# A Mamba layer on one core: ScalarE's carry copy and its exponential two states ahead, moved to the head of each slot

## The chip, the cores and the metric

One core of a Trainium2 chip runs the whole program. Its engines work side by side, each with a queue of its own that is executed in order: PE (TensorE, matrix products), DVE (VectorE), ACT (ScalarE), POOL (GpSimd), and SP (SyncE), which here only issues DMAs. They wait for one another through semaphores. The metric is the device time of one execution in microseconds, the median of several runs.

## The reference, cut to what matters

The input is x, 2 images of 512 channels x 4096 tokens in float32. Layer 0 is a group norm and a Mamba block, layer 1 a group norm and linear attention; both are residual. The change touches layer 0 only:

```
h0 = zeros                          # 1024 channels x 16 states
dA  = exp(d_t[..., None] * A)       # delta times A, for each channel and state
dBu = (d_t * u_t)[..., None] * b_t[:, None, :]
h   = dA * h + dBu
y   = einsum('bdn,bn->bd', h, c_t)
...
delta = softplus(dt @ dt_proj_w.T + dt_proj_b)
xn = (xf - mu) * rsqrt(var + EPS) * ln_w + ln_b
y = y * silu(z)
```

## The kernel before

**Tiling.** The 2 x 4096 tokens are cut into 16 chunks of T = 512 tokens. The 1024 inner channels are 8 tiles (j = 0 to 7) of 128 partitions, each with 16 states (n = 0 to 15). A chunk thus has 128 slots, slot = 16 j + n, and in each slot DVE runs one scan, `h = dA * h + dBu` along the 512 tokens of one tile and state (L638). Scan and slot have the same number here; "state 7 of tile 0" is slot 7. `chunk_loop` runs a body for chunks -1, 0, a loop over 1 to 14 (its body stands once in the program), 15 and 16. A body does three things at once: `scan` for chunk c, `front` for chunk c+1 (load of x, group norm, layer norm, input projection, convolution, softplus' input) and `project` for chunk c-1 (output projection, residual). Scan and front are both on for chunks 0 to 14.

**Order.** Every engine has a function of its own (`scalar_chunk`, `vector_chunk`, `gpsimd_chunk`, `tensor_chunk`) that walks through the 128 slots, and tables at the head of the file (NORM, RSTD = 24, NEWTON = 26, SP_LN = 5, Y_COPY = 2, and so on) say in which slot, or in which state of every tile, a piece of side work stands. So the queues' order is written by hand. Around a scan, in slot s:

- ACT (`scalar_chunk`) does the side work of the slot first. Then it copies the last column of scan s-1 into `carry` (L516; L520 for the first slot of a chunk), where the next chunk's scan of that tile and state begins; it waits for `h_ready`, that is for scan s-1. Then it computes exp(delta * A) for the scan of slot s+2 (L536), into SBUF (`da`, a ring of 3) or, for the six states whose dBu DVE computes, into one of three PSUM banks. The ring slot is free when scan s-1 is over, so this waits for the same scan.
- DVE does its side work, then the dBu product of the next state if that is one of the six (L625), then the scan. The scan waits for the exponential and for dBu.
- PE makes dBu for the other ten states, two slots ahead (L704, once scan s-1 is over), does its side work, and adds hc of slot s-2 into `y_ps` (L815).
- POOL multiplies each scan's result by C (L683: `hc`), between the sums of softplus and `du` (L651 to L669) and the gating (L676).

**ACT's side work**, with the lines of the profile:

- softplus for the next tile, in the states of each tile: Abs and Relu at 0 (L475, L479), Exp at 2 (L483), two roundings at 3 and 4 (L486, L490), Ln at 5 (L494). Ln lies in another table than Exp, so a table load stands before the Ln (L494) and another before the next exponential (L536);
- the copy of y out of PSUM at 2 (L506), which PE turns back (L713) for DVE's skip step (L594, state 4); before it PE must have summed state 15, and PE's sum of state 0 waits for the copy;
- the gate's Tanh at 9 (L510), between PE's product z (L787) and DVE's L588 (state 10); du_t at 13 (L498) and the copy of du at 15 (L502);
- for the next chunk: in slot 0 the issue of the load of x (L409), the group norm's scale at 4, 5, 9, 10 (L416), squares at 17 and 20 (L428), the layer norm's rstd as exp(-0.5 ln(var)) at 24 (L432, L434, with two table loads), which DVE refines by a Newton step at 26 (L552 to L560) and applies at 27 (L563); the affine step at 29 to 32 (L441); and for each of the eight tiles the convolution's first steps (L448 to L454) and its Tanh (L461), after PE's products (L757).

Slot 20 on DVE has the skip step of tile 0 and also adds the residual to one output tile (L601), with PE's output projection (L804, slots 0 to 36) behind both.

## Time and profile before

| | us |
|---|---|
| median of 3 runs | 5342.18 (5341.98 to 5363.9) |
| the profiled execution | 5340.43 |
| its span | 5338.7 |
| layer 0, scans of chunks 0 to 15 | from about 200 to about 4550 |
| layer 1 | the rest, to the end |

The page gives the busy time of each engine, the span in 40 slices and the costliest groups of instructions. Of the trace, these views are used: the waits (who waited for whom, in total), a table of busy times by stretch, and the instructions in order of time. There each row ends in brackets with the idle time of the engine just before it and what ended it. The granted TensorE clock is 0.97 over the span and 0.98 in the steady part of layer 0. One chunk takes 276 us there, and the chunks are alike.

### The profile page before, as it was taken

What the parts mean: (1) busy time and instruction counts of PE and PEld (TensorE: products, weight loads), DVE (VectorE), ACT (ScalarE), POOL (GpSimd) and SP (SyncE); (2) the same over time, 40 slices, a digit from 0 to 9 for tenths busy, and PEclk for the clock granted to TensorE, in tenths of its full rate; (3) what the DMA queues carried; (4) which work ended last, traced back from release to release, by engine and by line L of the source; (5) the groups of instructions that cost most, each with busy time, mean ns of one, the idle gap of its engine ahead of it and who ended that gap; (6) DMA issues with size and microseconds to landing.
All of it is one profiled execution on the core that took longest, in us unless ns stands there. A gap on an engine that the chain in (4) does not pass through costs nothing. (4 is left out here: it accounts for less than half of the span.)

```text
span 5338.7 us, 89822 instructions
## 1 busy us (share of the span) xinstructions
PE 4649.2 (87%) x26392; PEld 3406.2 (64%) x26392; DVE 3953.3 (74%) x4317; ACT 3672.1 (69%) x7235; POOL 3660.5 (69%) x2906
## 2 busy tenths in 40 slices
PE   2798989898989888989898989898898988798998
PEld 0566666666666666666666666666666667586786
DVE  4788878887888898888888888878788888212212
ACT  1677767677777776777777777767676767463563
POOL 1577777787777777777777787777777779332332
PEclk9999999999999999999999999999999999999999
DMA  5102020202020202010101010010102020322313
GB/s 188 52 2 68 2 67 3 65 5 65 5 65 5 61 9 61 9 57 13 57 13 57 13 39 31 28 42 12 58 2 68 1 64 1 111 67 92 113 56 110
DMA packets 119826, 245.63 MB, mean 46 GB/s; under 512 B 10496, under 2 KB 11648, under 8 KB 117728
## 3 DMA queue, kind: packets, MB, share of 16 engines
q1 hardware_dynamic: 110816, 222.30, 12.9%
q10 hardware_dynamic: 8448, 16.78, 0.9%
q8 instruction: 237, 3.88, 0.3%
q14 instruction: 325, 2.66, 0.2%
HBM read 204.44 MB, written 34.60 MB: 45 GB/s over the span
## 5 line engine op out<-in xcount | busy, mean ns | idle before, releaser
L683 POOL TENSOR_TENSOR hc<-hs,c_rows 128x512 f32<-128x512 f32 x2048 | 2626.2, 1299 | 996.9 <-DVE hs L638 930.9
L638 DVE TENSOR_TENSOR_SCAN hs<-da,carry,bank 128x512 f32<-128x512 f32 x1280 | 1623.0, 1268 | 133.0 <-PE bank L704 52.8
L704 PE MATMUL bank<-b_diag,du_t 128*128 128x128 f32 x10240 | 1414.1, 282 | 290.0 <-DVE hs L638 258.3
L815 PEld LDWEIGHTS bank<-identity,hc 128*128 128x128 f32 x8192 | 1010.6, 142 | 825.3 <-issue 720.2
L704 PEld LDWEIGHTS bank<-b_diag,du_t 128*128 128x128 f32 x10240 | 1269.4, 195 | 364.4 <-DVE hs L638 350.2
L815 PE MATMUL bank<-identity,hc 128*128 128x128 f32 x8192 | 1232.3, 276 | 58.7 <-ACT sp_l L506 39.4
L638 DVE TENSOR_TENSOR_SCAN hs<-bank,carry,hs 128x512 f32<-128x512 f32 x768 | 963.3, 1263 | 43.3 <-ACT bank L536 43.3
L536 ACT ACTIVATE da<-delta,neg_a 128x512 f32<-128x512 f32 x1280 | 910.7, 711 | 21.4 <-DVE hs L638 19.9
L516 ACT ACTIVATE carry<-hs,keep_now 128x1 f32<-128x1 f32 x2032 | 582.6, 287 | 327.1 <-DVE hs L638 320.9
L986 POOL TENSOR_TENSOR xg_low<-xg,xg_high 128x512 fp32r<-128x512 f32 x192 | 248.7, 1296 | 474.1 <-ACT xg_high L1010 466.6
L804 PE MATMUL bank<-xs,w_out 128*128 (+1 forms) x1024 | 520.5, 622 | 35.9 <-issue 34.3
L757 PE MATMUL bank<-xn,w_in 128*128 (+1 forms) x1024 | 524.8, 604 | 18.6 <-ACT xn L441 10.8
L625 DVE TENSOR_TENSOR hs<-bank,b_rows 128x512 f32<-128x512 f32 x768 | 518.2, 675 | 13.1 <-ACT carry L516 7.3
L787 PE MATMUL bank<-xn,w_in 128*128 (+1 forms) x1024 | 525.2, 595 | 0.0
L536 ACT ACTIVATE bank<-delta,neg_a 128x512 f32<-128x512 f32 x768 | 521.4, 679 | 0.5
L573 DVE SCALAR_TENSOR_TENSOR bank<-raw,w_conv,bank 128x512 f32<-128x512 f32 x384 | 288.4, 751 | 43.2 <-ACT bank L454 34.0
L804 PEld LDWEIGHTS bank<-xs,w_out 128*128 128x128 f32 x1024 | 180.7, 199 | 148.6 <-issue 143.5
L594 DVE SCALAR_TENSOR_TENSOR xs<-xs,skip,bank 128x512 f32 (+1 forms) x128 | 95.2, 744 | 220.8 <-PE bank L713 220.7
L651 POOL TENSOR_TENSOR sp_w<-sp_w,sp_e 128x512 f32<-128x512 f32 x128 | 163.4, 1276 | 136.0 <-ACT sp_w L490 136.0
L1010 ACT ACTIVATE xg<-xl,gn_bias,gn_scale 128x512 f32<-128x512 f32 x192 | 154.9, 807 | 138.3 <-DMA xl<-x 126.4
L510 ACT ACTIVATE zs<-bank 128x512 f32<-128x512 f32 x128 | 76.5, 597 | 233.9 <-PE bank L787 233.9
L1099 DVE COPY ek_t<-l_bank 128x512 f32<-128x512 f32 x64 | 44.3, 692 | 219.1 <-PE l_bank L1174 219.1
(157 smaller groups left out, 5987.8 us busy)
## 6 DMA issues: line engine op xcount, KB each, us to landing
c_rows<-b_and_c_rows SPq DMA_DIRECT2D x256, 256.0 KB, 3.4
xl<-x SPq DMA_DIRECT2D x48, 1024.0 KB, 5.6
b_rows<-b_and_c_rows SPq DMA_DIRECT2D x96, 256.0 KB, 3.7
c_rows<-in_x SPq DMA_DIRECT2D x8, 2048.0 KB, 8.5
xn<-in_x ACTq DMA_DIRECT2D x16, 1024.0 KB, 7.6
xres<-in_x SPq DMA_DIRECT2D x64, 256.0 KB, 2.9
x<-xres SPq DMA_DIRECT2D x64, 256.0 KB, 2.0
out<-keys SPq DMA_DIRECT2D x16, 1024.0 KB, 5.0
```

The costliest lines, as they stand in the source:

```text
L516: act.activation(carry[:, col:col + 1], hs[:, (n - 1) % H_RING, T - 1:T], ACT.Copy, scale=keep_now[:, 0:1]).then_inc(carried, 1)
L536: act.activation(x_ps[x][:, :] if nn in BY_VECTOR else da[:, x, :], delta[:, jn % 2, :], ACT.Exp, scale=neg_a[:, jn, nn:nn + 1]).then_inc( ...
L573: dve.scalar_tensor_tensor(in_ps[t % 2][:, :], raw[:, TAPS - 1 - s:TAPS - 1 - s + T], w, in_ps[t % 2][:, :], ALU.mult, ALU.add).then_inc(c ...
L625: dve.tensor_tensor(hs[:, nn % H_RING, :], du_ps[:, :], b_rows[:, v, :], ALU.mult).then_inc(dbu_ready, 1)
L638: dve.tensor_tensor_scan(hs[:, n % H_RING, :], decay, inflow, carry[:, STATE * j + n:STATE * j + n + 1], ALU.mult, ALU.add).then_inc(h_rea ...
L683: pool.tensor_tensor(hc[:, n % HC_RING, :], hs[:, n % H_RING, :], c_rows[:, n, :], ALU.mult).then_inc(hc_ready, 1)
L704: mm = pe.matmul(x_ps[target % STEPS % X_RING][:, q * P:(q + 1) * P], du_t[:, q * P:(q + 1) * P], b_diag[:, w, q, :], start=True, stop=True)
L757: mm = pe.matmul(in_ps[t % 2][:, :], w_in[:, ct, t * P:(t + 1) * P], xn[:, f % 2, ct, :], start=ct == 0, stop=ct == CT - 1)
L787: mm = pe.matmul(pb[:, :], w_in[:, ct, lo:lo + P], xn[:, c % 2, ct, :], start=ct == 0, stop=ct == CT - 1)
L804: mm = pe.matmul(out_ps[ct][:, :], w_out[:, k, ct * P:(ct + 1) * P], xs[:, o % 2, k, :], start=k == 0, stop=k == JT - 1)
L815: mm = pe.matmul(y_ps[:, q * P:(q + 1) * P], hc[:, ns % HC_RING, q * P:(q + 1) * P], identity[:, :], start=ns == 0 and q == 0, stop=ns == ...
L986: pool.tensor_tensor(xg_parts[1][:, u, ct, :], xg[:, ct % 2, :], xg_parts[0][:, u, ct, :], ALU.subtract).then_inc(lowered, 1)
```

## The change

In `scalar_chunk` a block of code moves from the end of the slot's body to its head: the copy of the carry, in slot 0 of a chunk also the copy of `keep_now` (L525), and the exponential for the slot two further on. The side work follows it. Nothing else is different: the same instructions, the same waits in front of each, and the queues of the other engines have the same rows as before.

```
@@ scalar_chunk, for each slot
                             step = STEPS * c + slot
+                            if scan and n > 0 or (j > 0 and scan):
+                                prev = step - 1
+                                col = STATE * j + n - 1
+                                act.wait_ge(h_ready, prev + 1)
+                                act.activation(carry[:, col:col + 1], hs[:, (n - 1) % H_RING, T - 1:T], ACT.Copy,
+                                               scale=keep_now[:, 0:1]).then_inc(carried, 1)
+                            if scan and j == 0 and n == 0 and not (isinstance(c, int) and c == 0):
+                                act.wait_ge(h_ready, step)
+                                act.activation(carry[:, STEPS - 1:STEPS], hs[:, H_RING - 1, T - 1:T], ACT.Copy,
+                                               scale=keep_now[:, 0:1]).then_inc(carried, 1)
+                            if (scan or front) and j == 0 and n == 0:
+                                wait(act, carried, STEPS * c)
+                                wait(act, halo_saved, JT * f)
+                                act.activation(keep_now[:, :], keep[:, bass.ds(c + 1, 2)], ACT.Copy).then_inc(keep_set, 1)
+                                act.wait_ge(keep_set, c + 2)
+
+                            target = slot + 2
+                            if scan if target < STEPS else front:
+                                jn, nn = target // STATE % JT, target % STATE
+                                if nn == 0:
+                                    act.wait_ge(delta_ready, tile + 2)
+
+                                wait(act, h_ready, step + (target % STEPS < X_RING - 1))
+                                x = target % STEPS % X_RING
+                                act.activation(x_ps[x][:, :] if nn in BY_VECTOR else da[:, x, :], delta[:, jn % 2, :],
+                                               ACT.Exp, scale=neg_a[:, jn, nn:nn + 1]).then_inc(da_ready, 1)
                             if front and slot == 0:
                                 wait(act, z_mm, JT * c)
...
                                 act.activation(zs[:, :], pb[:, :], ACT.Tanh).then_inc(tanh_z, 1)
...
```

(The same lines are taken away after the last line shown.) The line numbers move with it: L516 becomes L410, L536 becomes L430, and the side work's lines grow by 26.

**ACT in the loop's chunk, slots 21 to 24 of tile 1.** `da` and `bank1` are exponentials, `carry` the copies, `sp_l` the softplus Ln, and the last rows rstd. Before:

```order
L494 ACT_TABLE_LOAD
L494 ACTIVATE sp_l<-sp_e,units 128x512
L515 REGISTER_ALU
L516 ACTIVATE carry<-hs,keep_now 128x1
L536 ACT_TABLE_LOAD
L536 ACTIVATE da<-delta,neg_a 128x512
L515 REGISTER_ALU
L516 ACTIVATE carry<-hs,keep_now 128x1
L536 ACTIVATE bank1<-delta,neg_a 128x512
```

and after:

```order
L410 ACTIVATE carry<-hs,keep_now 128x1
L430 ACTIVATE da<-delta,neg_a 128x512
L520 ACT_TABLE_LOAD
L520 ACTIVATE sp_l<-sp_e,units 128x512
L409 REGISTER_ALU
L410 ACTIVATE carry<-hs,keep_now 128x1
L430 ACT_TABLE_LOAD
L430 ACTIVATE bank1<-delta,neg_a 128x512
```

The Ln of slot 21 stood ahead of that slot's carry and exponential, and now stands behind them; the second table load now precedes the exponential into `bank1` (state 8) instead of the one into `da` (state 7).

**ACT, slots 23 and 24 of tile 1, up to rstd's Exp.** Before:

```order
L516 ACTIVATE carry<-hs,keep_now 128x1
L536 ACTIVATE da<-delta,neg_a 128x512
L431 REGISTER_ALU
L432 ACT_TABLE_LOAD
L432 ACTIVATE sq<-bank5,eps 128x512
L433 ISA
L434 ACT_TABLE_LOAD
L434 ACTIVATE sq<-sq 128x512
```

and after:

```order
L410 ACTIVATE carry<-hs,keep_now 128x1
L430 ACTIVATE da<-delta,neg_a 128x512
L409 REGISTER_ALU
L410 ACTIVATE carry<-hs,keep_now 128x1
L430 ACTIVATE da<-delta,neg_a 128x512
L457 REGISTER_ALU
L458 ACT_TABLE_LOAD
L458 ACTIVATE sq<-bank5,eps 128x512
L459 ISA
L460 ACT_TABLE_LOAD
L460 ACTIVATE sq<-sq 128x512
```

Carry and exponential of slot 24 now stand ahead of rstd as well.

**ACT, slots 0 and 1 of the loop's chunk.** Before:

```order
L409 DMA xn<-in_x 128x4x512
L473 REGISTER_ALU
L53 REGISTER_ALU
L475 ACTIVATE sp_e<-bank6,b_dt 128x512
L53 REGISTER_ALU
L479 ACTIVATE delta<-bank6,b_dt 128x512
L519 REGISTER_ALU
L520 ACTIVATE carry<-hs,keep_now 128x1
L53 REGISTER_ALU
L525 ISA
L525 ACTIVATE keep_now<-keep 128x2
L526 REGISTER_ALU
```

and after:

```order
L414 ACTIVATE carry<-hs,keep_now 128x1
L53 ISA
L419 ISA
L419 ACTIVATE keep_now<-keep 128x2
L420 REGISTER_ALU
L430 ACTIVATE bank3<-delta,neg_a 128x512
L53 REGISTER_ALU
L435 ISA x2
L435 DMA xn<-in_x 128x4x512
L499 REGISTER_ALU
L53 REGISTER_ALU
L501 ACTIVATE sp_e<-bank6,b_dt 128x512
```

The exponential into `bank3` (state 2) stood behind the last row shown of before; now it comes ahead of the load of x and of the softplus steps.

## Rows read from the trace of the kernel before

**Rows 1.** The page: busy time of each engine, and one row of the DMA issues.
```profile
PE 4649.2 (87%) x26392; PEld 3406.2 (64%) x26392; DVE 3953.3 (74%) x4317; ACT 3672.1 (69%) x7235; POOL 3660.5 (69%) x2906
...
xn<-in_x ACTq DMA_DIRECT2D x16, 1024.0 KB, 7.6
```

**Rows 2.** Busy times by stretch: tiles 0, 1 and 7 of one chunk.
```profile
2373.70:2412.40 38.70, 37.07 (x208) 25.99 (x208) 29.47 (x30) 27.64 (x55) 26.66 (x22) 0.99 0.23 78
2410.60:2452.30 41.70, 36.56 (x210) 25.56 (x209) 34.10 (x35) 31.61 (x59) 29.92 (x22) 1.00 0.06 20
...
2615.90:2647.00 31.10, 22.68 (x161) 18.41 (x161) 29.16 (x35) 21.49 (x43) 27.29 (x22) 1.00 0.53 158
```
The columns of rows 2 are: stretch, its length, busy time (and count) of PE, PEld, DVE, ACT and POOL, granted clock, DMA share, GB/s.

**Rows 3.** Waits of DVE, 300 to 4400 us: total, times, longest.
```profile
DVE xs L594 <- PE bank L713: 214.5, 104, 3.7
DVE zs L588 <- ACT zs L510: 139.2, 90, 2.4
DVE hs L638 <- ACT carry L516: 46.3, 42, 1.4
...
DVE hs L638 <- ACT bank L536: 42.7, 15, 4.0
...
DVE sq L552 <- ACT sq L434: 14.8, 14, 1.1
```

**Rows 4.** Waits of ACT in the same stretch.
```profile
ACT zs L510 <- PE bank L787: 220.5, 104, 4.4
```

**Rows 5.** ACT in order of time, slots 21 to 23 of tile 1: start, duration.
```profile
2421.95 1.28 ACT L494 ACT_TABLE_LOAD   x1
2423.24 0.72 ACT L494 ACTIVATE sp_l<-sp_e,units 128x512 f32<-128x512 f32 x1
2424.36 0.29 ACT L516 ACTIVATE carry<-hs,keep_now 128x1 f32<-128x1 f32 x1 [0.40 <-DVE hs L638]
...
2426.60 0.28 ACT L516 ACTIVATE carry<-hs,keep_now 128x1 f32<-128x1 f32 x1
...
2427.40 0.28 ACT L516 ACTIVATE carry<-hs,keep_now 128x1 f32<-128x1 f32 x1
```

**Rows 6.** DVE in order of time, tile 0 of the same chunk.
```profile
2379.93 1.28 DVE L638 TENSOR_TENSOR_SCAN hs<-bank,carry,hs 128x512 f32<-128x512 f32 x1 [3.15 <-ACT bank L536]
...
2384.43 0.75 DVE L594 SCALAR_TENSOR_TENSOR xs<-xs,skip,bank 128x512 f32 x1 [2.05 <-PE bank L713]
```

**Rows 7.** In order of time, states 7 and 10 of tile 4.
```profile
2531.44 1.28 DVE L638 TENSOR_TENSOR_SCAN hs<-da,carry,bank 128x512 f32<-128x512 f32 x1 [1.16 <-ACT carry L516]
...
2535.66 0.69 DVE L588 SCALAR_TENSOR_TENSOR zs<-zs,bank 128x512 f32<-128x512 f32 x1 [0.59 <-ACT zs L510]
```

**Rows 8.** In order of time, tile 5: scan 81, copy of y, PE's sum behind it.
```profile
2551.95 1.27 DVE L638 TENSOR_TENSOR_SCAN hs<-da,carry,bank 128x512 f32<-128x512 f32 x1
...
2553.06 0.59 ACT L506 ACTIVATE sp_l<-bank 128x512 f32<-128x512 f32 x1
...
2555.13 0.60 PE L815 MATMUL bank<-identity,hc 128*128 128x128 f32 x4
```

**Rows 9.** In order of time, tile 7: scan 113, copy of y, sum, skip step.
```profile
2618.23 1.27 DVE L638 TENSOR_TENSOR_SCAN hs<-da,carry,bank 128x512 f32<-128x512 f32 x1
...
2618.82 0.60 ACT L506 ACTIVATE sp_l<-bank 128x512 f32<-128x512 f32 x1 [0.22 <-PE bank L815]
...
2620.55 0.60 PE L815 MATMUL bank<-identity,hc 128*128 128x128 f32 x4
...
2622.36 0.72 DVE L594 SCALAR_TENSOR_TENSOR xs<-xs,skip,bank 128x512 f32 x1
```

**Rows 10.** DVE in order of time, tile 1: slot 20 and slot 26.
```profile
2420.35 0.75 DVE L594 SCALAR_TENSOR_TENSOR xs<-xs,skip,bank 128x512 f32 x1 [3.69 <-PE bank L713]
...
2432.27 1.35 DVE L552 TENSOR_TENSOR sq<-sq 128x512 f32<-128x512 f32 x1 [1.06 <-ACT sq L434]
```

**Rows 11.** PE in order of time, tile 1, after scan 26.
```profile
2439.15 1.16 PE L704 MATMUL bank<-b_diag,du_t 128*128 128x128 f32 x8 [1.43 <-DVE hs L638]
```

More of the change, by code:

```diff
@@ L510, in scalar_chunk @@
                                 act.activation(zs[:, :], pb[:, :], ACT.Tanh).then_inc(tanh_z, 1)
-                            if scan and n > 0 or (j > 0 and scan):
-                                prev = step - 1
-                                col = STATE * j + n - 1
-                                act.wait_ge(h_ready, prev + 1)
-                                act.activation(carry[:, col:col + 1], hs[:, (n - 1) % H_RING, T - 1:T], ACT.Copy,
-                                               scale=keep_now[:, 0:1]).then_inc(carried, 1)
-                            if scan and j == 0 and n == 0 and not (isinstance(c, int) and c == 0):
-                                act.wait_ge(h_ready, step)
-                                act.activation(carry[:, STEPS - 1:STEPS], hs[:, H_RING - 1, T - 1:T], ACT.Copy,
-                                               scale=keep_now[:, 0:1]).then_inc(carried, 1)
-                            if (scan or front) and j == 0 and n == 0:
-                                wait(act, carried, STEPS * c)
-                                wait(act, halo_saved, JT * f)
-                                act.activation(keep_now[:, :], keep[:, bass.ds(c + 1, 2)], ACT.Copy).then_inc(keep_set, 1)
-                                act.wait_ge(keep_set, c + 2)
-                            target = slot + 2
-                            if scan if target < STEPS else front:
-                                jn, nn = target // STATE % JT, target % STATE
-                                if nn == 0:
-                                    act.wait_ge(delta_ready, tile + 2)
-                                wait(act, h_ready, step + (target % STEPS < X_RING - 1))
-                                x = target % STEPS % X_RING
-                                act.activation(x_ps[x][:, :] if nn in BY_VECTOR else da[:, x, :], delta[:, jn % 2, :],
-                                               ACT.Exp, scale=neg_a[:, jn, nn:nn + 1]).then_inc(da_ready, 1)
                 def vector_chunk(dve, c, scan, front, project):
```

## The prediction, as it was put on record

> **What bounds the kernel now.** I began with the busy shares: PE is busy for 87% of the span, DVE 74%, ACT and POOL 69% each [rows 1]. No engine is full, so the waits decide. I then cut one chunk of the steady part (the one from 2373.7 us) at its eight tiles [rows 2]. A tile takes 31 to 42 us. PE and DVE share the bound: in tile 0 PE is busy for 37.1 of 38.7 us, in tile 7 DVE for 29.2 of 31.1 us. Tile 1 is the longest, with 5.1 us of idle on PE and 7.6 on DVE. In the waits of DVE [rows 3] the two large entries are the skip step waiting for PE's transpose of y (214.5 us over 4100 us of the layer) and the gate step waiting for ACT's tanh (139.2 us). The scans' two large waits for ACT's carries and exponentials make 46.3 + 42.7 = 89 us; that is about what the change can give back on DVE. ACT itself waits for PE at its side work, the most before the gate tanh: 220.5 us, 104 times [rows 4].
>
> **What the change is, seen on ACT's queue.** Before, the queue reads side(s), carry(s), exp(s), side(s+1). Now it reads carry(s), exp(s), side(s), carry(s+1). No instruction is added or dropped; all side work simply stands one carry-exp pair later. A pair takes 0.80 us from its start to the next one's (2426.60 to 2427.40 in [rows 5]). The carry of slot s waits for the end of scan s-1, so all side work of a slot now waits for that scan too. Before, side(s) could start as soon as scan s-2 was over and exp(s-1) issued.
>
> **Gain: exponentials that wait behind side work.** (a) State 2 of tile 0. After the loop's jump ACT issues the load of x, two softplus steps and then the exponential; scan 2 waits 3.15 us for it [rows 6], and this is most of the 42.7 us. It will come some 2 us earlier. But 4 us later DVE waits again, 2.05 us for PE at the skip step [rows 6], and PE is busy for 37.1 of 38.7 us in this tile [rows 2]. Worth 0: DVE only reaches the next PE wait sooner. (b) State 7, behind the Ln and the two table loads around it: 1.16 us of wait in tile 4, but 4 us later DVE waits 0.59 us more for the tanh [rows 7], one of the 104 tanhs that had themselves waited for PE [rows 4]. So this is also worth 0, and at most the 46.3 us of its row in [rows 3] if I misjudge PE.
>
> **Loss that can be absorbed.** Where ACT waits for PE before side work (before the tanh in 104 of the some 118 tiles of that stretch [rows 4]), the pair of 0.80 us slips into that wait and the side work starts when it did. The copy of y is the case to look at, because in tiles 5 to 7 ACT does not wait for PE. In tile 5 it started at 2553.06; now the carry before it waits for scan 81 to end at 2553.22, then 0.80 for the pair and 0.52 for the softplus step: 2554.54, so 1.5 later, done at 2555.1. PE reads it at 2555.13 [rows 8]. Worth 0, by a hair. In tile 7 scan 113 ends at 2619.50, the copy ends at 2621.4 instead of 2619.42, and PE wanted it at 2620.55: 0.9 us late on PE. PE's transpose of y comes next, so y is back at about 2622.5, and DVE's skip step started at 2622.36 without a wait [rows 9]. I take 0.1 us a chunk, with 0.9 as its upper end. The load of x is issued behind the first pair of the chunk, so about one pair later, and lands 7.6 us after its issue [rows 1]. ACT's first normalisation, at slot 4, may now wait for it; but the next pair, slot 5's, needs scan 4, which DVE runs only after its wait for PE at the skip step [rows 6], so that is 0 too.
>
> **Loss that is not absorbed: the layer norm's rstd in tile 1.** This is the term of the sum. At slot 21 ACT does a table load and the softplus Ln, at slot 24 two table loads around Ln and Exp for rstd, and DVE's Newton step at slot 26 waits for that Exp in every chunk already (1.06 us [rows 10]; 14 times out of 14 in [rows 3]). In tile 1 DVE is held 3.69 us at slot 20 by PE. Before, ACT used this pause: the Ln of slot 21 ran from 2421.95 to 2423.96, and the carry of slot 21 started at 2424.36, when scan 20 ended [rows 5]. Now the Ln of slot 21 may only start after that carry and its exponential. From the same start, 2424.36, ACT has to do, ahead of rstd's Exp, everything that it did before, plus the table load and Ln (1.28 + 0.72 = 2.00 us) and one more pair (0.80 us), the one of slot 24. So the Exp ends 2.8 us later, at about 2435.0 instead of 2432.23.
> DVE waits for it with nothing else to do (its queue is in order: behind the Newton steps stand the gate, a dBu product and scan 26). Its wait grows from 1.06 to 3.9 us less what scans 24 and 25 are late themselves. Is there slack behind? PE already waits 1.43 us for scan 26 [rows 11], so it hangs on that scan and loses what DVE loses; ACT's next carry and POOL's next product hang on it too. The whole 2.8 us moves on. Fifteen chunks have scan and layer norm together (chunk -1 norms alone, chunk 15 scans alone): 15 x 2.8 = 42 us.
> What a table switch costs decides how much of the pause is used up. In [rows 5] a load is 1.28 us, is followed by its activation 0.01 us later, and nothing else shows.
> The Trainium skill ("ScalarE: Activation LUTs", What ACT_TABLE_LOAD costs) adds a drain of about 1380 ns to 1283 ns of load, 2.66 us a switch. This trace shows only the load. By the page the old Ln would have ended about 1 us after scan 20, and the same sum would give 2.66 + 0.72 + 0.80 - 1.0 = 3.2 us a chunk, 48 us in all.
>
> **The sum.** The profiled execution took 5340.4 us (its span 5338.7), the median of the runs is 5342.2. Gains 0; rstd +42; tile 7's y +1.5 (15 x 0.1); layer 1 is untouched. 5340.4 + 43.5 = 5383.9, and the runs' median lies 1.8 us above the profiled execution: 5386.
>
> **Rivals.**
> *Faster: the exponentials do bound.* If DVE rather than PE sets tiles 0, 3 and 4, the 89 us of waits for exponentials and carries come back while rstd still costs 42: 5342 - 89 + 42 = 5295. For it: these waits stand on DVE, which idles little in the tiles without output projection (tile 7 in [rows 2]). Against it: [rows 6] and [rows 7], where DVE runs into a PE wait within a few us. It wins if PE has idle time after the state-7 scans; there it has none.
> *About the same.* The state-7 waits come back (42 of them in the 14 chunks of [rows 3], so three tiles a chunk; the two outside tile 0 make 30 us) and cancel most of rstd: 5342 + 43 - 30 = 5355. Or the pause at slot 26 lets POOL and PE catch up. Chance higher, as this needs only one misread tile.
> *Much slower: y and Ln late in all DVE-bound tiles.* The copy of y is 1.5 us later in tiles 5 and 6 and 2.0 in tile 7, and the Ln now starts behind carry and exponential in every tile, so that the exponential of state 8, not 7, comes last (by the steps of [rows 5], about 0.5 us late in tiles 5 and 6). If PE cannot hide these, each chunk loses 1.5 + 1.5 + 2.0 + 1.0 = 6 us more, 90 us: 5475. For it: tile 5's copy has no margin. Against: in tile 6 the x-projection stands ahead of PE's read. It starts to count as soon as the copy comes over 0.1 us later than I reckon.
> *The change does nothing*: the order on ACT does change, so this exists only as the same-case above.
>
> **Chances and range.** Forecast (own range 5368 to 5405) 0.52; about the same 0.22; much slower, part or all, 0.16; faster 0.10. The range has to reach to two of the rivals: 5338 to 5450; it leaves out the full slower case and the faster one. A difference under 0.5% (27 us) can't be told from none here, so faster (under 5315) is 0.11, the same (5315 to 5369) is 0.24 and slower is 0.65; the forecast lies 17 us above that line.
>
> **What would show it.** Right: DVE's Newton step waits about 3.5 us for rstd's Exp, 15 times (50 to 60 us in its row, from 14.8 over 14 times); the first pair of slot 21 still starts at scan 20's end; tile 1 is near 44.5 us, the other tiles within 0.5 us of before; waits of scans for ACT at state 2 and 7 are gone, with DVE's waits for PE's transpose and for the tanh up by as much. Wrong: tile 1 unchanged (then something hides rstd); tiles 5 to 7 longer with PE waiting for the copy of y (then slower); tiles 0, 3 or 4 shorter (then faster).

## The result, and the profile after

| | before | after |
|---|---|---|
| median of the runs, us | 5342.08 (10 runs, 5327.76 to 5363.9) | 5379.41 (10 runs, 5360.02 to 5384.62) |
| ratio | | 1.0061, 95% interval 1.0042 to 1.0079 |
| span of the profiled execution, us | 5338.7 | 5377.1 |

The changed kernel is 0.6% slower. All ratios, here and below, are taken against runs of the kernel before made beside those of the other kernel (their medians lie between 5337 and 5343 us), and they differ by up to 0.0015 from the quotient of the two medians. The page of after has as many instructions on each engine as before [rows 1]. What grew most on it is the idle time of ACT before the carry copy, 843.6 us where it was 327.1:

```profile
PE 4672.5 (87%) x26392; PEld 3419.5 (64%) x26392; DVE 3939.4 (73%) x4317; ACT 3693.0 (69%) x7235; POOL 3652.0 (68%) x2906
...
L410 ACT ACTIVATE carry<-hs,keep_now 128x1 f32<-128x1 f32 x2032 | 588.1, 289 | 843.6 <-DVE hs L637 838.4
```

The waits of the steady part (300 to 4400 us: total, times, longest) answer to [rows 3] and [rows 4]:

```profile
DVE xs L593 <- PE bank L712: 230.5, 118, 3.7
DVE zs L587 <- ACT zs L536: 134.6, 89, 2.4
DVE hs L637 <- ACT bank L430: 88.3, 89, 3.2
...
DVE sq L551 <- ACT sq L460: 42.5, 14, 3.0
...
DVE hs L637 <- ACT carry L410: 0.8, 1, 0.8
```
```profile
ACT zs L536 <- PE bank L786: 114.3, 102, 3.0
```

The scans' wait for carries is gone (46.3 us, now 0.8); it stood at state 7 alone. Their wait for exponentials in a bank has doubled (42.7, now 88.3), and it stands elsewhere. Before, 42.2 us of it were at state 2 of tile 0. Now 15.2 us are at state 2 and 72.0 at state 8, whose exponential, instead of state 7's, stands behind the Ln. All waits of scans for ACT make 91.7 us before and 96.0 after, so the change gave nothing of them back in sum. The wait for the skip step is 16.0 us up. The Newton step waits 3.0 us in each of the 14 chunks instead of 1.1.

Three tiles of the chunk that answers to [rows 2], tiles 0, 1 and 7 (stretch, its length, busy time and count of PE, PEld, DVE, ACT and POOL, granted clock, DMA share, GB/s):

```profile
2392.24:2431.08 38.84, 35.56 (x185) 23.63 (x184) 27.65 (x28) 25.22 (x49) 24.99 (x20) 0.96 0.25 80
2431.08:2474.11 43.03, 38.48 (x201) 26.60 (x200) 31.82 (x34) 29.80 (x55) 28.55 (x21) 0.92 0.04 14
...
2640.21:2672.45 32.24, 22.91 (x161) 18.47 (x161) 29.41 (x34) 21.96 (x43) 27.32 (x22) 1.00 0.48 157
```

One chunk is not enough here, since some tiles have a short and a long form. So the table takes the mean length of each tile over chunks 1 to 14, from the start of its first scan to the start of the next tile's. Tile 2 is 32.70 in all kernels and is left out. The kernels below the first two are the experiments of the next section.

| us a chunk | tile 0 | 1 | 3 | 4 | 5 | 6 | 7 | chunk | ratio to before |
|---|---|---|---|---|---|---|---|---|---|
| before | 38.65 | 41.74 | 31.60 | 32.76 | 32.55 | 35.83 | 31.13 | 276.96 | |
| after | 38.83 | 42.60 | 31.29 | 33.24 | 33.08 | 35.83 | 31.63 | 279.20 | 1.0061 |
| undo_both | 39.00 | 41.79 | 31.27 | 32.64 | 33.08 | 35.83 | 31.65 | 277.95 | 1.0037 |
| alone | 38.99 | 42.65 | 31.61 | 33.12 | 32.66 | 35.83 | 31.33 | 278.90 | 1.0041 |
| undo_y | 38.69 | 42.70 | 31.21 | 31.49 | 32.93 | 35.71 | 31.25 | 276.68 | 1.0008 |
| fill_before | 39.09 | 41.92 | 31.60 | 33.01 | 32.85 | 34.74 | 31.31 | 277.21 | 1.0007 |
| fill_after | 38.98 | 45.11 | 31.28 | 33.01 | 32.85 | 35.79 | 31.64 | 281.35 | 1.0150 |
| mix | 39.97 | 41.86 | 31.21 | 31.49 | 33.64 | 35.84 | 31.27 | 277.97 | 1.0018 |
| fill_mix | 39.41 | 41.88 | 31.21 | 33.01 | 32.85 | 35.19 | 31.20 | 277.44 | 1.0018 |
| fill82_mix | 38.90 | 41.58 | 31.21 | 31.49 | 32.85 | 34.63 | 31.20 | 274.56 | 0.9925 |
| best | 38.47 | 40.71 | 31.21 | 31.50 | 32.86 | 34.27 | 31.12 | 272.83 | 0.9937 |
| fill82_before | 39.31 | 41.63 | 31.60 | 32.52 | 32.85 | 35.81 | 31.21 | 277.64 | 1.0025 |

The lengths are those of the one profiled execution of each kernel, the ratio is that of all its runs. For best the profiled execution is its fastest run (5283.93 us), so its row looks better than its ratio.

After minus before is +2.24 us a chunk, and 14 chunks of it are 31 of the 38.4 us between the two spans. Tile 1 has 0.86 of it, where the prediction had nearly all of it. Tiles 4, 5 and 7 have 0.5 each, tile 0 has 0.2, and tile 3 gives 0.3 back.

### The profile page after: what moved, and what is told of

It reads as the page before. It is cut to its first block and busy times, and to the rows that moved or that the text cites. A ratio compares the mean times of both kernels' runs of the same rounds, so it can differ in the third digit from the quotient of the medians.

```text
span 5377.1 us, 89822 instructions
## 1 busy us (share of the span) xinstructions
PE 4672.5 (87%) x26392; PEld 3419.5 (64%) x26392; DVE 3939.4 (73%) x4317; ACT 3693.0 (69%) x7235; POOL 3652.0 (68%) x2906
## 5 line engine op out<-in xcount | busy, mean ns | idle before, releaser
L682 POOL TENSOR_TENSOR hc<-hs,c_rows 128x512 f32<-128x512 f32 x2048 | 2621.2, 1296 | 1040.0 <-DVE hs L637 976.6
L637 DVE TENSOR_TENSOR_SCAN hs<-da,carry,bank 128x512 f32<-128x512 f32 x1280 | 1624.7, 1269 | 91.7 <-PE bank L703 79.8
L410 ACT ACTIVATE carry<-hs,keep_now 128x1 f32<-128x1 f32 x2032 | 588.1, 289 | 843.6 <-DVE hs L637 838.4
L430 ACT ACTIVATE da<-delta,neg_a 128x512 f32<-128x512 f32 x1280 | 911.3, 712 | 26.1 <-DVE hs L637 26.1
L430 ACT ACTIVATE bank<-delta,neg_a 128x512 f32<-128x512 f32 x768 | 521.9, 680 | 2.0
L756 PEld LDWEIGHTS bank<-xn,w_in 128*128 128x128 f32 x1024 | 163.4, 196 | 52.1 <-issue 27.7
```

The lines of the kernel that those rows point to most:

```text
L410: act.activation(carry[:, col:col + 1], hs[:, (n - 1) % H_RING, T - 1:T], ACT.Copy, scale=keep_now[:, 0:1]).then_inc(carried, 1)
L430: act.activation(x_ps[x][:, :] if nn in BY_VECTOR else da[:, x, :], delta[:, jn % 2, :], ACT.Exp, scale=neg_a[:, jn, nn:nn + 1]).then_inc( ...
L637: dve.tensor_tensor_scan(hs[:, n % H_RING, :], decay, inflow, carry[:, STATE * j + n:STATE * j + n + 1], ALU.mult, ALU.add).then_inc(h_rea ...
L682: pool.tensor_tensor(hc[:, n % HC_RING, :], hs[:, n % H_RING, :], c_rows[:, n, :], ALU.mult).then_inc(hc_ready, 1)
L756: mm = pe.matmul(in_ps[t % 2][:, :], w_in[:, ct, t * P:(t + 1) * P], xn[:, f % 2, ct, :], start=ct == 0, stop=ct == CT - 1)
```

## The experiments

### The two pieces in tile 1, taken back and done alone

**undo_both** is the changed kernel with two pieces ahead of carry and exponential again: the Ln of slot 21 and rstd at slot 24.

```
+                            if front and slot == RSTD:
+                                ...  (rstd, moved up)
+                            if (front if j == 7 else scan) and n == SP_LN and j == 1:
+                                wait(act, y_back, tile)
+                                act.activation(sp_l[:, :], sp_e[:, :], ACT.Ln, bias=one).then_inc(sp_ln, 1)
                             if scan and n > 0 or (j > 0 and scan):
...
-                                if n == SP_LN:
+                                if n == SP_LN and j != 1:
```

> The changed kernel with two pieces of side work put back ahead of the carry-exponential pair: the softplus Ln of slot 21 and rstd's Ln and Exp of slot 24. Everything else stays moved. Theory (these two pieces are what makes tile 1 longer): DVE's wait for rstd's Exp falls from 3.0 us to about 1.1, the Newton steps take their old time, scan 24 no longer waits 1.2 us for its exponential, and tile 1 without clock falls is back from 42.3 to 40.8 us, so about 15 x 1.5 = 22 us less than the changed kernel: 5357, if the TensorE clock falls as often. Rival (the slowdown is in the copy of y and in tiles 4, 5 and 7, tile 1 is not worth anything): within 5 us of 5379. Rival (all of it is where the TensorE clock happens to fall): tile 1 keeps its length in the chunks where the clock stays up.

Measured: 5363.42 us, ratio 1.0037 (1.0023 to 1.0050). Tile 1 is as before (41.79), but tiles 5 and 7 stay where the change had put them. The two pieces account for some 13 us (1.0061 less 1.0037; with both intervals, 1 to 25); some 20 us of the loss lie elsewhere.

**alone** is the kernel before with the opposite edit: only these two pieces stand behind carry and exponential.

> The kernel before with only those two pieces moved behind the pair (softplus Ln of slot 21, rstd of slot 24). Theory: this alone gives tile 1 its new length, rstd's Exp at 24.5 us after scan 16, DVE waiting 3.0 us for it, tile 1 up by 1.5 us in chunks without a clock fall, all other tiles as before: 5342 + 22 = 5364, give or take the clock. Rival (the clock alone): tile 1 as before, 5342. Rival (all 2.8 us arrive): 5384.

Measured: 5366.4 us, ratio 1.0041 (1.0025 to 1.0056), so 22 us (13 to 30). Tile 1 is 42.65, as in after. Another 0.4 us came in tile 4 and 0.3 in tile 0, where none of its instructions had moved. That was the first hint at the clock, below.

**undo_ln21** takes back only the Ln of slot 21.

> The changed kernel with only the softplus Ln of slot 21 put back ahead of its pair; rstd stays behind the pair of slot 24. If both parts of the 2.8 us are as I added them (2.0 for table load and Ln, 0.8 for the pair), rstd's Exp ends 0.8 us later than in the kernel before when measured from the start of tile 1 (22.5 us after scan 16's start, against 21.7 before and 24.5 after). Rival (the pair of slot 24 is hidden): 21.7. Scan 24's wait for its exponential is gone by both.

Measured: 5370.97 us (a single run), tile 1 at 42.0 us in 13 of 14 chunks. The Exp ended 22.8 us after scan 16's start.

### Where 1.35 of rstd's 2.85 us went

ACT in after, slots 21 to 24 of tile 1 (start, duration). The scan of slot 16 starts at 2431.08 here and at 2410.58 before.

```profile
2444.87 0.30 ACT L410 ACTIVATE carry<-hs,keep_now 128x1 f32<-128x1 f32 x1 [3.22 <-DVE hs L637]
2445.07 0.71 ACT L430 ACTIVATE da<-delta,neg_a 128x512 f32<-128x512 f32 x1
2445.80 1.28 ACT L520 ACT_TABLE_LOAD   x1
2447.09 0.73 ACT L520 ACTIVATE sp_l<-sp_e,units 128x512 f32<-128x512 f32 x1
...
2454.96 0.63 ACT L460 ACTIVATE sq<-sq 128x512 f32<-128x512 f32 x1
```

The carry starts when scan 20 ends, the Ln comes behind the pair, and rstd's Exp ends at 2455.59. That is 24.51 us after scan 16's start. Before, it ended 21.66 after it: DVE's Newton step started at 2432.27 [rows 10]. So the Exp is 2.85 us late; the prediction said 2.8. DVE in order of time, after:

```profile
2450.14 1.28 DVE L637 TENSOR_TENSOR_SCAN hs<-bank,carry,hs 128x512 f32<-128x512 f32 x1 [1.19 <-ACT bank L430]
...
2455.62 0.95 DVE L551 TENSOR_TENSOR sq<-sq 128x512 f32<-128x512 f32 x1 [3.03 <-ACT sq L460]
2456.61 0.69 DVE L553 SCALAR_TENSOR_TENSOR sq<-bank,sq 128x512 f32<-128x512 f32 x1
2457.33 0.66 DVE L556 TENSOR_SCALAR sq<-sq 128x512 f32<-128x512 f32 x1
2458.02 0.69 DVE L559 TENSOR_TENSOR sq<-sq 128x512 f32<-128x512 f32 x1
```

and the last two Newton steps before (the first is in [rows 10]: 1.35 us):

```profile
2434.38 0.66 DVE L557 TENSOR_SCALAR sq<-sq 128x512 f32<-128x512 f32 x1
2435.07 1.64 DVE L560 TENSOR_TENSOR sq<-sq 128x512 f32<-128x512 f32 x1
```

The first and the last step read two operands from SBUF. They took 1.35 and 1.64 us before, and take 0.95 and 0.69 after. From the first start to the end of the fourth the chain was 4.44 us and is 3.09. The other engine at work in that stretch is POOL. Before, it had four products to do beside the chain (three are shown), and after, it runs out of them, since scan 26 is late:

```profile
2431.79 1.28 POOL L655 TENSOR_TENSOR delta<-delta,sp_l 128x512 f32<-128x512 f32 x1
...
2434.71 1.46 POOL L660 TENSOR_TENSOR delta<-delta,sp_w 128x512 f32<-128x512 f32 x1
2436.13 1.73 POOL L683 TENSOR_TENSOR hc<-hs,c_rows 128x512 f32<-128x512 f32 x1
```
```profile
2454.75 1.28 POOL L659 TENSOR_TENSOR delta<-delta,sp_w 128x512 f32<-128x512 f32 x1
2455.98 1.73 POOL L682 TENSOR_TENSOR hc<-hs,c_rows 128x512 f32<-128x512 f32 x1
```

The first fence is before, where POOL is busy to 2437.86; the second is after, where its last product ends at 2457.71 and DVE's last step starts at 2458.02.

The rows also show how. A step that meets a product of POOL in flight does not run at a lower speed, it waits for the end of that product. L655's product ends at 2433.07, and L552 at 2433.62; L660's ends at 2436.17, and L560 at 2436.71; in after L659's ends at 2456.03, and L551 at 2456.57. So it is in every one of chunks 1 to 14 of before, after and undo_ln21: the step ends 0.55 us after the product. The other way round, a product of POOL that starts while such a step is on is the one that is longer: 1.73 us instead of 1.28 for L682, which starts at 2455.98 under L551.

**short_pool** tests this: the kernel before, with POOL's product cut to one column in slots 22 to 26.

```
-                                pool.tensor_tensor(hc[:, n % HC_RING, :], hs[:, n % H_RING, :], c_rows[:, n, :],
-                                                   ALU.mult).then_inc(hc_ready, 1)
+                                wide = 1 if front and 22 <= slot <= 26 else T
+                                pool.tensor_tensor(hc[:, n % HC_RING, :wide], hs[:, n % H_RING, :wide],
+                                                   c_rows[:, n, :wide], ALU.mult).then_inc(hc_ready, 1)
```

> The kernel before, with POOL's product hc made over 1 column instead of 512 in slots 22 to 26 of tile 1 of chunks that have a front part; y of those states is left out, so the output is wrong there and PE sums old values. It asks why the Newton steps (four on DVE) took 4.45 us before and 3.10 after. Theory (DVE's products of two SBUF operands are slowed by POOL's): with POOL nearly idle they take 0.7 + 0.7 + 0.7 + 0.7 = about 3 us, the first and the last step, 1.35 and 1.64 us before, falling below 1 us. Rival (their length has to do with ACT or with table loads): 1.35 and 1.64 us stay.

Measured: 5323.7 us (a single run, and of a kernel that leaves work out, so its time is no price of anything). DVE in short_pool:

```profile
2428.85 0.69 DVE L552 TENSOR_TENSOR sq<-sq 128x512 f32<-128x512 f32 x1 [1.07 <-ACT sq L434]
2429.57 0.69 DVE L554 SCALAR_TENSOR_TENSOR sq<-bank,sq 128x512 f32<-128x512 f32 x1
2430.30 0.43 DVE L557 TENSOR_SCALAR sq<-sq 128x512 f32<-128x512 f32 x1
2430.76 0.69 DVE L560 TENSOR_TENSOR sq<-sq 128x512 f32<-128x512 f32 x1
```

The chain is 2.60 us, with the same wait for the Exp ahead of it (1.07 us). So POOL's products beside it are what stretches it. (Tile 1 is 37.9 us, 2.9 less than the short form of before and more than the chain's 1.8; where the rest comes from stays open.) The Trainium skill ("SBUF — State Buffer", Who interferes with whom) says which steps to expect this of: a DVE instruction with two SBUF inputs contends with a GpSimd instruction that reads SBUF, and one with at most one SBUF input, outside the two-port modes, does not. The rows agree for the two long steps and for L554, which has one operand in PSUM (0.69 in all three kernels). L557 reads one SBUF operand and still is longer beside POOL: 0.66 us before and in after, where POOL is at work until 0.28 us before its end, against 0.43 in short_pool. It is a tensor_scalar, and the same section counts that among the operations that can enter a two-port mode and so contend.

In undo_ln21 the two pieces can be read apart. There the Exp was only 1.1 us late, POOL was still at work, and nothing came back:

```profile
2444.62 1.46 DVE L554 TENSOR_TENSOR sq<-sq 128x512 f32<-128x512 f32 x1 [2.16 <-ACT sq L463]
...
2447.53 1.64 DVE L562 TENSOR_TENSOR sq<-sq 128x512 f32<-128x512 f32 x1
```

Scan 26 starts 28.47 us after scan 16 in undo_ln21, 28.75 in after, 27.26 before. So the late rstd alone, 1.1 us on the Exp, made the scan 1.2 us late. The second piece (the late Ln, 1.7 us on the Exp) thus added only 0.3 us to the scan.

### The copy of y

**undo_y** is the changed kernel, but in state 2 of every tile the side work stands ahead of carry and exponential.

```
+                            late = n == Y_COPY
+                            if not late:
+                                pair()          # carry, exponential
                             ...                 # side work
+                            if late:
+                                pair()
```

> The changed kernel, but in state 2 of each tile the side work (the copy of y, and in slot 2 softplus' Exp step with it) stands ahead of carry and exponential again; Ln, rstd and everything else stay behind them. If the late copy of y is what costs tile 7 its 0.5 us and sets off some of the clock falls of tiles 4 and 5: tile 7 31.2 to 31.3 us, tile 4 at 32.3 in most chunks, tile 1 stays at 42.3 to 43.0, the time some 10 to 15 us below the changed kernel, 5365 to 5370. If the copy is harmless, as my prediction had it for tiles 5 and 6 and nearly for tile 7: tile 7 stays at 31.7, time within 5 us of the changed kernel (5379).

Measured: 5343.03 us, ratio 1.0008 (0.9992 to 1.0024). **With rstd still late, nearly the whole loss is gone.** The copy of y is worth 28 us in the changed kernel (1.0061 less 1.0008; with both intervals, 15 to 41), more than the 10 to 15 I had put down for it and far more than the 1.5 of the prediction. By the table 1.75 of the 2.5 us a chunk are in tile 4 and 0.4 in tile 7. But undo_y is not before again: its tile 1 is still 0.96 us longer than before, and its tiles 4 and 3 are 1.27 and 0.39 shorter. A loss and a gain cancel in it. Tile 4 shows how. PE's sum behind the copy, in tile 4 of chunk 8, in before, after and undo_y:

```profile
2523.01 0.63 PE L815 MATMUL bank<-identity,hc 128*128 128x128 f32 x4 [2.52 <-ACT sp_l L506]
```
```profile
2545.46 0.80 PE L814 MATMUL bank<-identity,hc 128*128 128x128 f32 x4 [2.53 <-ACT sp_l L532]
```
```profile
2527.11 0.63 PE L821 MATMUL bank<-identity,hc 128*128 128x128 f32 x4 [1.72 <-ACT sp_l L537]
```

PE waits 2.5 us for the copy before and after, and 1.7 us in undo_y. The reason is in ACT's rows of undo_y and of after:

```profile
2525.05 0.30 ACT L411 ACTIVATE carry<-hs,keep_now 128x1 f32<-128x1 f32 x1
2525.24 0.72 ACT L431 ACTIVATE da<-delta,neg_a 128x512 f32<-128x512 f32 x1
2525.85 0.63 ACT L514 ACTIVATE sp_e<-sp_e 128x512 f32<-128x512 f32 x1
2526.37 0.59 ACT L537 ACTIVATE sp_l<-bank 128x512 f32<-128x512 f32 x1
```
```profile
2542.80 0.72 ACT L430 ACTIVATE da<-delta,neg_a 128x512 f32<-128x512 f32 x1
2543.41 0.29 ACT L410 ACTIVATE carry<-hs,keep_now 128x1 f32<-128x1 f32 x1
2543.60 0.72 ACT L430 ACTIVATE da<-delta,neg_a 128x512 f32<-128x512 f32 x1
2544.21 0.63 ACT L509 ACTIVATE sp_e<-sp_e 128x512 f32<-128x512 f32 x1
2544.73 0.59 ACT L532 ACTIVATE sp_l<-bank 128x512 f32<-128x512 f32 x1
```

Pair first lets slot 64's pair run ahead of that slot's convolution steps, so one pair less is left in front of the copy: a gain of 0.8 us (the copy starts 5.82 us into the tile, against 6.62 before and in after). In after, slot 66's own pair is put in front of the copy, which takes the gain away again. In undo_y the gain stays, and tile 4 is 31.5 us in all 14 chunks. In before and after it is 32.3 or 34.0. Here are tile 4 in a long and in a short form of after, and in undo_y:

```profile
2538.10:2572.07 33.97, 31.03 (x186) 23.10 (x186) 30.11 (x35) 26.99 (x58) 26.79 (x23) 0.95 0.01 1
...
2816.88:2849.17 32.29, 29.16 (x185) 21.84 (x185) 30.10 (x34) 26.99 (x58) 26.70 (x23) 1.00 0.01 1
```
```profile
2520.54:2552.04 31.50, 28.80 (x182) 21.48 (x182) 30.00 (x35) 26.94 (x58) 26.67 (x23) 1.00 0.01 1
```

In the long form the granted clock is 0.95 and PE is busy 1.9 us more with the same work. Its sum behind the 2.53 us wait takes 0.80 instead of 0.63 us. So 0.8 of the 1.75 us in tile 4 are the copy's own, and the rest are falls that no longer come.

In tile 7 PE waits 0.88 us for the copy in after and DVE 0.37 us for the skip step, where it did not wait before [rows 9]; undo_y takes this back (31.25). PE and DVE in after:

```profile
2645.95 0.63 PE L814 MATMUL bank<-identity,hc 128*128 128x128 f32 x4 [0.88 <-ACT sp_l L532]
```
```profile
2647.18 0.75 DVE L593 SCALAR_TENSOR_TENSOR xs<-xs,skip,bank 128x512 f32 x1 [0.37 <-PE bank L712]
```

### The granted clock

In before, the granted clock falls from full (2.4 GHz) to half (1.2 GHz) for a stretch in tile 6 of every chunk and, in some chunks, in tiles 0, 1, 4 and 5 and in the last slot of tile 7. Where I looked, PE had waited just before. Tile 1 of chunks 8 and 9 of before, short and long:

```profile
2410.58:2451.35 40.77, 35.63 (x201) 24.63 (x200) 33.17 (x34) 30.80 (x57) 29.14 (x21) 1.00 0.04 15
2685.65:2728.12 42.47, 37.33 (x201) 25.38 (x200) 33.18 (x35) 30.92 (x57) 29.14 (x21) 0.96 0.04 14
```

One fall costs its tile 1.7 us. Over chunks 1 to 14 there are 48 stretches at half clock in before (170.7 us in all) and 57 in after (225.3 us). Tile 4 has its long form in 4 of 14 chunks before and in 8 after, tile 5 also in 4 and 8. In after, every chunk has one behind scan 26, where PE's wait grew from the 1.43 us of [rows 11] to 2.93, and the product behind it takes 2.07 instead of 1.16 us:

```profile
2461.16 2.07 PE L703 MATMUL bank<-b_diag,du_t 128*128 128x128 f32 x8 [2.93 <-DVE hs L637]
```

That fall lies beside DVE's 2.27 us multiplication L562, and costs little: the short length of tile 1 is 42.3 us, 1.5 more than before, and that is what scan 26 is late. PE's next wait, for POOL's du in slot 28, takes it up: it shrinks from 2.08 to 0.48 us. The later fall in tile 1, which cost 1.7 us in 8 of 14 chunks before, is rarer and shorter after (it lengthens the tile in 5 chunks, by 0.7 us in four of them). So of the 1.5 us that scan 26 is late, the mean of tile 1 shows 0.86.

Three kernels fill PE's waits: in slots 28, 66 and 82 it does four more products of 128x128x512, written over by what follows. Shown is one of the three places.

```
+                            if scan and front and slot == 82:
+                                pe.wait_ge(xs_ready, JT * f + 5)
+                                for _ in range(FILL):
+                                    pe.matmul(pa[:, :], w_in[:, 0, 0:P], xn[:, f % 2, 0, :], start=True, stop=True)
```

**fill_before** adds them to the kernel before, **fill_after** to the changed kernel.

> The kernel before, with 4 extra 512-column products on PE in each of three places where PE waits (ahead of the sum of slot 66, ahead of the product of slot 82, ahead of du's transpose in slot 28); their result is overwritten. It asks whether the two lengths that tiles 1, 4 and 5 show in the same kernel (40.8 or 42.5, 32.3 or 33.9, 32.1 or 33.7 us) come from the TensorE clock, which falls to half in some chunks after PE has waited there. Theory: with PE busy in these waits the clock stays up, the long variants vanish from tiles 4 and 5 and most of tile 1, worth some 1.6 us in 5 to 8 chunks of 14 for each tile: 25 to 30 us faster, 5315. Rival (the long variants come from something else, or the products delay PE): no change or slower, 5342 to 5360.

Measured: 5346.66 us, ratio 1.0007 (0.9988 to 1.0026), a miss. Tiles 1, 4 and 5 now have one length each: 41.9, 33.0 and 32.8 us. Before, they had two, 40.8 or 42.5, 32.3 or 34.0, 32.1 or 33.7. So the two lengths are the clock's. But the products cost 0.7 to 1.1 us where no fall would have come, and nothing is won in sum. Tile 6, ahead of which they also stand, is down to 34.1 us in 9 of 14 chunks.

> The changed kernel with the same 12 extra products a chunk. With the clock's falls gone from both, the difference of this kernel and fill_before is the change's own: by the tiles of the two traces +1.5 in tile 1, -0.3 in tile 3, +0.2 in tile 5, +0.5 in tile 7, about 1.9 us a chunk or 28 us. If instead the change only moved the clock's falls about, the two are within 8 us of each other.

Measured: 5422.01 us, ratio 1.0150 (1.0118 to 1.0182), a miss. Tiles 4 and 5 are 33.0 and 32.8 as in fill_before, but tile 1 is 45.1 us, and tile 6 keeps its fall in every chunk. PE in slot 28 of fill_after, and in the same slot of before:

```profile
2482.07 3.60 PE L723 MATMUL bank<-xn,w_in 128*128 x8
```
```profile
2443.69 0.66 PE L720 MATMUL bank<-identity,du 128*128 128x128 f32 x4 [2.08 <-POOL du L669]
```

The four products take 3.60 us at a granted clock of 1.00, the same as in fill_before; the fall behind scan 26 is over when they start (nearly over in some other chunks). What differs is the wait that they fill. Before, PE waits 2.08 us in slot 28 for POOL's du. In after it waits 0.48 us there, on average of the chunks, since the half-clock products behind scan 26 have taken up the rest. So here nearly all of their time is added to the tile (45.1 us against 42.3), and they stand too late to stop the fall behind scan 26. Products put where PE hardly waits only cost their time.

### Putting the pieces together

**mix** is the changed kernel with the side work first in states 2 and 5 of every tile and in slot 24, and the pair first elsewhere (`late = n in (Y_COPY, SP_LN) or slot == RSTD`). **fill_mix** adds the products of slots 28, 66 and 82.

> The changed kernel, but with the side work ahead of the pair in states 2 and 5 of every tile and in slot 24 (copy of y, softplus Ln, rstd), and the pair ahead everywhere else. Theory (these three are the pieces whose consumer waits or which belong in DVE's pause): tiles 1, 5 and 7 go back to 40.8, 32.1 and 31.2 us, the early exponential of slot 0 stays: 5342, within 10 us of the kernel before. Rival (moving the other side work costs too): 5350 to 5379.

Measured: 5353.21 us, ratio 1.0018 (0.9998 to 1.0037), just outside what I had expected. Tile 4 gains 1.3 us against before, but tiles 0 and 5 have more or longer falls (tile 5 is 33.8 us in 13 of 14 chunks), and give it back.

> mix with the 12 extra products. If both theories hold, as fast as fill_before, 5315, within 8 us; faster than it only if pairs ahead of the waits for PE are worth anything once the clock stays up.

Measured: 5350.23 us, ratio 1.0018 (0.9998 to 1.0039), a miss; one of its twelve runs took 15703.49 us and is not in the ratio. The products mend tile 5 (32.8, 0.8 less) and cost 1.5 us in tile 4 (33.0 instead of 31.5), which had no falls to mend.

So the products belong only where a fall comes in nearly every chunk, ahead of a wait of PE. **fill82_mix** keeps those of slot 82 alone.

> The mixed order (side work first in states 2 and 5 and in slot 24, carry and exponential first elsewhere) with four extra products on PE in slot 82 alone, written over by what follows, so that nothing of the result changes. From the tiles of the two earlier runs: tile 4 as without the extra products (31.5), tile 5 32.8 instead of 33.8 and tile 6 34.1 to 35.7 as with them, so 1.0 to 2.5 us less a chunk than the mixed order, 15 to 37 us: 5316 to 5338, level with or below the kernel before. If the clock falls only move to the next wait of PE, tiles 5 and 6 stay at 66.6 in sum or more and the time is 5345 to 5355.

Measured: 5305.11 us, ratio 0.9925 (0.9906 to 0.9943). This is faster than both kernels, and below the range I had given. Tiles 4 and 5 are as expected and tile 6 is 34.1 us in 10 of 14 chunks.

**best** puts the Ln of the other seven tiles behind the pair again (`late = n == Y_COPY or slot in (STATE + SP_LN, RSTD)`).

> The changed kernel with three pieces of ScalarE's side work ahead of carry and exponential again (the copy of y in state 2 of every tile, the Ln of slot 21 and rstd at slot 24) and the four extra products on PE in slot 82, written over by what follows. It differs from fill82_mix only in that the Ln of the other seven tiles stays behind the pair. If that Ln is harmless either way: 5305, the tiles as in fill82_mix (31.5, 32.8 and 34.1 in most chunks for tiles 4 to 6). If the Ln behind the pair costs the exponential of state 8 in every tile (my rival 'much slower'): some 0.5 us more in tiles 5 to 7 each, 5325.

Measured: 5308.37 us, ratio 0.9937 (0.9919 to 0.9954), with runs from 5283.93 to 5324.21. It can't be told from fill82_mix. In its trace tiles 5, 6 and 7 are as in fill82_mix where the clock stays up (32.9, 34.1 and 31.1 to 31.2), so a late Ln is harmless there.

**fill82_before** is the kernel before with the products of slot 82 alone.

> The kernel before with only the four extra products on PE in slot 82. It tells how much of the gain of fill82_mix is the products' and how much the order's. From the tiles of earlier runs (tile 4 32.7 as before, tile 5 32.8 instead of 32.6, tile 6 34.1 to 34.7 instead of 35.8) I expect 0.9 us less a chunk, 14 us: 5325, ratio 0.9975. If the whole gain is the products', it is at 5300 and tile 4 is at 32.3 in all chunks; if it is the order's alone, it is at 5337 or above and tile 6 is at 35.8.

Measured: 5356.62 us, ratio 1.0025 (1.0013 to 1.0036), a miss. Tile 6 stays at 35.81. Neither the mixed order nor the products of slot 82 gain by themselves, but both together gain 0.7%. Of the 3.1 us a chunk between fill82_before and fill82_mix, tile 4 has 1.0 and tile 3 has 0.4, mostly the order's, tile 0 has 0.4, and tile 6 has 1.2, which is the clock's. Tile 6 of chunk 8 in best and in fill82_before:

```profile
2554.80:2588.95 34.15, 30.01 (x189) 22.16 (x187) 28.11 (x31) 25.34 (x52) 25.78 (x22) 1.00 0.01 3
```
```profile
2589.34:2625.17 35.83, 31.68 (x189) 22.96 (x187) 28.00 (x32) 25.76 (x53) 25.78 (x22) 0.95 0.01 3
```

In both PE waits 2.41 us for DVE's scan some 3 us into the tile. Behind that wait the same dBu product keeps the full clock in best and slows in fill82_before (1.05 for seven of its eight parts and 1.16 for all, against 1.47):

```profile
2560.14 1.05 PE L715 MATMUL bank<-b_diag,du_t 128*128 128x128 f32 x7 [2.41 <-DVE hs L645]
```
```profile
2594.68 1.47 PE L709 MATMUL bank<-b_diag,du_t 128*128 128x128 f32 x8 [2.41 <-DVE hs L639]
```

Why the same wait makes it fall in one kernel and not in the other stays open. What PE did in the tiles ahead differs, and no run here separates that. It is not the order of ACT alone: in fill_before, with the order of before and products also in slots 28 and 66, 9 of 14 chunks are free of the fall.

## Why the prediction was right in sum and not in its parts

The forecast was 5386 us and the time is 5379.41. The sum had one large term, and the runs show that this is luck as well as reading: that term was 20 to 29 us too large, and the copy of y, which stood at 1.5 us, made up for it.

- **rstd in tile 1.** The mechanism and the place were right: the first pair of slot 21 starts at scan 20's end, and the Exp comes 2.85 us late against 2.8. The step that failed is "the whole 2.8 us moves on". At scan 26 only 1.5 us arrive, as the Newton chain behind the Exp got 1.35 us shorter, and the mean of tile 1 grew by 0.86 to 42.60, not to 44.5. The term of 42 us measured 13 (undo_both) to 22 us (alone). The rival "about the same" had the cause in a half-sentence ("lets POOL and PE catch up"), without a price of its own. Newton's row is 42.5 us over 14 times; I had said 50 to 60. Part of the Exp's lateness is taken by scan 24, which waits 1.19 us for the exponential of state 8 where it had not waited. A table load is again 1.28 us with the activation 0.01 us behind it. The drain that the Trainium skill ("ScalarE: Activation LUTs", What ACT_TABLE_LOAD costs) adds does not show in this case's traces.
- **The copy of y, "worth 0, by a hair" in tile 5, 0.1 us in tile 7.** This is the step that failed most: undo_y measures the copy at 28 us. In tile 5 it was nearly right: without a fall the tile is 32.1 us before and in undo_y, and 32.3 in after. In tile 7 it was in the middle of my range (0.5 us, upper end 0.9). In tile 4 I had not looked at it at all. There it cancelled a gain, and kept the 2.5 us wait on PE behind which the clock fell, in 8 of 14 chunks (4 before, with the same wait). The rival "much slower" had named the copy, with "tile 5's copy has no margin", but gave it chance only as a whole.
- **Gains worth 0.** State 2 of tile 0 is right: the scan's wait for the exponential fell from 3.0 to 1.1 us a chunk, and DVE waits as much later, for PE at state 3 and for the exponential of state 8 (2 us a chunk in tile 0). State 7 is not quite: its wait came back at state 8, but tile 3 is 0.3 us shorter, and tile 4 has 0.8 us to give once the copy of y is left where it was. The rival "about the same" rested on this.
- **Pairs that slip into ACT's waits for PE.** Right: ACT's wait before the gate's tanh fell from 220.5 to 114.3 us while DVE's wait for that tanh stayed (139.2 and 134.6). The load of x cost nothing either: ACT waited for it once in the steady part, for 2.6 us, and twice before, for 2.8 us in all.
- **Late Ln in tiles 5 to 7** (part of "much slower"): refuted by best against fill82_mix.
- **The clock** was in no term. Of the 38.4 us between the spans it has a part in tiles 4 and 5, where the undisturbed lengths of before and after are equal or 0.2 us apart and only the number of falls differs. In tile 1 it worked the other way and hid 0.6 of the 1.5 us.

By the ratios the parts, 13 + 28 us, are within the intervals of the whole, 33 us. By the tiles they are more than the whole (1.25 + 2.52 us a chunk against 2.24), since undo_y sets a gain free that the change as a whole did not show, and each kernel also changes how often the clock falls.

## What to carry to other kernels

When work moves in an in-order queue, list who reads each moved result in every tile, not only in the one with the largest wait; a gain and a loss of one pair's length can cancel in one tile and show as "no change". A delay does not arrive whole if the steps behind it are held up by a neighbour that the delay starves. And read the granted clock stretch by stretch: where a tile has two lengths, count how often each occurs before crediting the difference to the change.

## What the runs showed of the hardware

- A DVE step on two SBUF operands of 128x512 that meets a product of POOL waits for the product's end: it ended 0.55 us after it each time, and took 0.95 to 1.64 us, against 0.69 without POOL. A step with one PSUM operand stays at 0.69. A product of POOL that starts under such a step took 1.73 us against its usual 1.28.
- A wait of PE of 2 to 3 us can cost more than its length: the granted clock falls to half behind it, and the fall costs 1.7 us where PE is on the path (tiles 1, 4 and 5), next to nothing where PE has another wait soon behind it (tile 1 of after, behind scan 26).
- The scatter of the runs of one kernel goes with the falls. Among the runs of before that were timed beside best, those with a mean clock of 0.974 or 0.975 took 5327.51 to 5333.37 us, and those with 0.971 took 5350.23 to 5354.96.
- A few extra products in PE's wait paid for themselves only where a fall came nearly every time: 0.7% in the mixed order with those of slot 82 alone. In the order before, neither all three places (1.0007) nor slot 82 alone (1.0025) gained.
